# Projections, output weights, gate, up and down in four tiles of 32 columns of TensorE's array

## The reference, cut to what matters

```
x = x + attention(layernorm(x))
x = x + ffn(layernorm(x))

attention: q, k, v = split_heads(x @ W.T + b)       # 16 heads of 16
           q, k = rope(q), rope(k)
           att = softmax(causal mask of q @ k.T / 4)
           (att @ v) @ Wo.T + bo
ffn:       gate, up = fp4_linear(x, w_gate), fp4_linear(x, w_up)     # 256 -> 704
           fp4_linear(silu(gate) * up, w_down)                       # 704 -> 256
fp4_linear(x, w): both rounded to an FP4 grid in blocks of 16, then x @ w.T
```

## Time and profile before

| | us |
|---|---|
| median of 3 runs | 1334.23 |
| the profiled execution's own time | 1329.79 |
| its span, first to last instruction | 1327.6 |
| TensorE (PE) busy | 1266.5 |
| VectorE (DVE) busy | 1088.6 |
| ScalarE (ACT) busy | 792.5 |
| GpSimd (POOL) busy | 472.1 |

### The profile page before, as it was taken

How to read it: one execution, slowest core, us unless ns; L and a number is a source line. 1 busy time by engine, 2 the same in 40 slices (tenths; PEclk the granted TensorE clock), 3 DMA queues, 4 the chain that set the end, 5 groups by cost and what they waited for, 6 DMA issues and landing times.

```text
span 1327.6 us, 43992 instructions
## 1 busy us (share of the span) xinstructions
PE 1266.5 (95%) x19062; PEld 821.1 (62%) x19062; DVE 1088.6 (82%) x2242; ACT 792.5 (60%) x1691; POOL 472.1 (36%) x499
## 2 busy tenths in 40 slices
PE   7679999999999999999999999999999999999967
PEld 6456555555666775666576766566765676855445
DVE  5788898989899897986468979889998898984256
ACT  5346667666567665675655647555665585766621
POOL 2944664653112203113355651313122312023346
PEclk9879999999999999999999999999999999999989
DMA  4634132202110110101023222111100100000000
GB/s 107 171 93 114 51 86 70 80 19 58 34 34 2 42 27 18 27 3 43 13 66 90 62 67 57 34 34 34 26 18 26 42 2 14 7 1 18 13 13 16
DMA packets 56988, 57.54 MB, mean 43 GB/s; under 512 B 10062, under 2 KB 50384, under 8 KB 56784
## 3 DMA queue, kind: packets, MB, share of 16 engines
q1 hardware_dynamic: 55496, 53.66, 15.0%
q10 hardware_dynamic: 1300, 1.08, 0.3%
HBM read 37.55 MB, written 16.78 MB: 41 GB/s over the span
## 4 chain that ended last, share of the span: by engine, by line
PE 76%; DVE 15%; ACT 3%; POOL 3%; issue 2%; DMA 1%; SPq 0%; ACTq 0%; POOLq 0%; DVEq 0%
PE bank L906 16%; PE bank L860 15%; PE bank L883 14%; PE bank L918 13%; DVE piece_max L1282 7%; PE bank L1038 5%; PE bank L978 4%; ACT prob L1182 2%; PE bank L986 2%; PE bank L1029 1%; PE bank L913 1%; PE bank L887 1%; PE bank L866 1%; DVE c_mem L1354 1%; DVE c_mem L1344 1%
## 5 line engine op out<-in xcount | busy, mean ns | idle before, releaser
L1182 ACT ACTIVATE prob<-bank 128x512 f32<-128x512 f32 (+3 forms) x1280 | 605.2, 539 | 280.5 <-PE bank L883 160.2
L1282 DVE TENSOR_REDUCE piece_max<-bank 128x1 f32<-128x512 f32 (+3 forms) x1120 | 690.3, 662 | 26.3 <-PE bank L860 11.9
L860 PE MATMUL bank<-k_mem,q_mem 96*32 96x512 bf16 (+3 forms) x5120 | 441.2, 351 | 7.3 <-DVE piece_max L1282 4.8
L883 PE MATMUL bank<-q_mem,k_mem 99*32 99x512 bf16 (+3 forms) x5120 | 443.6, 349 | 4.3 <-DVE piece_max L1282 2.4
L906 PE MATMUL bank<-prob,V 128*32 128x512 f32 (+3 forms) x2560 | 309.2, 531 | 6.6 <-ACT prob L1182 6.0
L883 PEld LDWEIGHTS bank<-q_mem,k_mem 99*32 99x32 bf16 x5120 | 190.2, 96 | 124.0 <-issue 63.1
L860 PEld LDWEIGHTS bank<-k_mem,q_mem 96*32 96x32 bf16 x5120 | 188.5, 97 | 116.3 <-issue 63.5
L1490 POOL TENSOR_TENSOR c_mem<-c_mem 128x256 f32<-128x256 f32 (+2 forms) x74 | 85.5, 1156 | 474.9 <-DVE c_mem L1366 474.9
L887 PE MATMUL bank<-mask_kq,ident_h 128*32 128x128 bf16 (+3 forms) x2048 | 129.8, 200 | 0.0
L866 PE MATMUL bank<-mask_qk,ident_h 128*32 128x32 bf16 (+3 forms) x2048 | 116.6, 203 | 0.0
L906 PEld LDWEIGHTS bank<-prob,V 128*32 128x32 f32 x2560 | 84.4, 110 | 42.0 <-ACT prob L1182 17.6
(11 more groups left out here) (174 smaller groups left out, 1412.8 us busy)
## 6 DMA issues: line engine op xcount, KB each, us to landing
parts_dram<-a_mem SPq DMA_DIRECT2D x13, 512.0 KB, 3.3
q_mem<-parts_dram SPq DMA_DIRECT2D x32, 192.0 KB, 2.9
k_mem<-parts_dram SPq DMA_DIRECT2D x32, 192.0 KB, 3.5
q_mem<-parts_dram SPq DMA_DIRECT2D x32, 128.0 KB, 3.1
k_mem<-parts_dram SPq DMA_DIRECT2D x32, 128.0 KB, 3.4
c_mem<-in_L_attn_x SPq DMA_DIRECT2D x30, 128.0 KB, 2.1
out<-c_mem SPq DMA_DIRECT2D x30, 128.0 KB, 1.7
a_mem<-in_L_attn_x SPq DMA_DIRECT2D x13, 256.0 KB, 2.6
```

Source lines behind the costliest of these rows:

```text
L860: m = pe.matmul(b[q0:q0 + COLUMNS, j * keys:(j + 1) * keys], q_rows(u)[0:TERM_ROWS, h, i * P + q0:i * P + q0 + COLUMNS], k_rows(k0 // CHUN ...
L883: mm = pe.matmul(b[k0:k0 + COLUMNS, off:CHUNK], k_rows(j // TPC, g)[:, h, first:first + COLUMNS], q_rows(u)[:, h, off:CHUNK], start=True, ...
L1182: act.activation(prob[:, n % NP, off:CHUNK], bank_of("st", n)[:, off:CHUNK], ACT.Exp, scale=SCALE).then_inc(drained("st", n)[0], 1)
L1282: dve.tensor_reduce(piece_max[:, u % 2, h0:h0 + len(heads), slot], src.rearrange("p (h k) -> p h k", k=keys), AX.X, ALU.max).then_inc(drai ...
```

## The change

The five products that had a stationary operand of 128 columns are written as four matmuls with 32 columns each, for each of their parts of the contraction. The streamed operand of the four is the same, and each writes its own 32 partitions of the bank. The planner is told that these jobs are `divided`. The durations that it takes for them are left as they are, and so are all transposes, which it takes as not divided, the one of the maxima too.

```
-        plan.start(plan.through(("v", z), 1728, "dve", 600, [...], [("past v",), ("v bias load",)]), pair_sooner(z))
+        plan.start(plan.through(("v", z), 1728, "dve", 600, [...],
+                                [("past v",), ("v bias load",)], divided=True), pair_sooner(z))
...   (q and k, wo, g0, g1, u0, u1 and down: divided as well)
             def product(b, src, w, lo, width):
                 for d in range(DK):
-                    m = pe.matmul(b[:, 0:width], src[:, d * P:(d + 1) * P], w[:, d, lo:lo + width],
-                                  start=(d == 0), stop=(d == DK - 1))
+                    for t0 in range(0, P, COLUMNS):
+                        m = pe.matmul(b[t0:t0 + COLUMNS, 0:width], src[:, d * P + t0:d * P + t0 + COLUMNS],
+                                      w[:, d, lo:lo + width], start=(d == 0), stop=(d == DK - 1))
                 return m
...   project_features
-                    for d in range(DK):
-                        m = pe.matmul(b[:, a * SIDE:(a + 1) * SIDE], WqkvT[:, d, o * D + a * P:o * D + (a + 1) * P],
+                    for d, f0 in ((d, f0) for d in range(DK) for f0 in range(0, P, COLUMNS)):
+                        of = o * D + a * P + f0
+                        m = pe.matmul(b[f0:f0 + COLUMNS, a * SIDE:(a + 1) * SIDE], WqkvT[:, d, of:of + COLUMNS],
                                       A[a_set[z]]["xnT"][:, d, :], start=(d == 0), stop=(d == DK - 1))
...   project_v: the same over i and d
...   down
-                for j in range(len(DOWN)):
-                    m = pe.matmul(b[:, 0:D], hT[0:DOWN[j], j * P:(j + 1) * P], WdT[0:DOWN[j], j, :],
-                                  start=(j == 0), stop=(j == len(DOWN) - 1))
+                for j, t0 in ((j, t0) for j in range(len(DOWN)) for t0 in range(0, P, COLUMNS)):
+                    m = pe.matmul(b[t0:t0 + COLUMNS, 0:D], hT[0:DOWN[j], j * P + t0:j * P + t0 + COLUMNS],
+                                  WdT[0:DOWN[j], j, :], start=(j == 0), stop=(j == len(DOWN) - 1))
```

More of the change, by code:

```diff
@@ L309, in rehearse_projection @@
                                     [("drain", "bias")] + old("lo"),
-                                    ("act", (name + "0", z), 285, ("drain", "bias"), *old("lo"))), pair_sooner(z))
+                                    ("act", (name + "0", z), 285, ("drain", "bias"), *old("lo")), True), pair_sooner(z))
         plan.start(plan.through(("v", z), 1728, "dve", 600, [("drain", "xnT", z), ("drain", "aw", 2)],
-                                [("past v",), ("v bias load",)]), pair_sooner(z))
+                                [("past v",), ("v bias load",)], divided=True), pair_sooner(z))
         for n, name in enumerate(("cos load", "sin load")):
@@ L472, in rehearse_feed_forward @@
         yield from plan.step("pool", ("residual", t), 685, [("f x load", t), ("bo load",)])
-        yield from plan.through(("wo", t), 864, "dve", 342, [("drain", "yT", t)], [("residual", t)])
+        yield from plan.through(("wo", t), 864, "dve", 342, [("drain", "yT", t)], [("residual", t)], divided=True)
         yield from plan.step("dve", ("f stats", t), 335, [("drain", "wo", t)])
@@ L482, in rehearse_feed_forward @@
             yield from plan.through((f"g{half}", t), 1184, "dve", 430, [("drain", "xT", t)], [],
-                                    ("act", ("tanh", half, t), 360) + ((("drain", "g0", t),) if half else ()))
-            yield from plan.through((f"u{half}", t), 1184, "dve", 435, [("drain", "xT", t)], [("drain", f"g{half}", t)])
+                                    ("act", ("tanh", half, t), 360) + ((("drain", "g0", t),) if half else ()), True)
+            yield from plan.through((f"u{half}", t), 1184, "dve", 435, [("drain", "xT", t)], [("drain", f"g{half}", t)], divided=True)
         yield from rehearse_rounding(("h", t), FF, [("drain", "u1", t)])
@@ L487, in rehearse_feed_forward @@
         yield from plan.through(("hT1", t), 220, "act", 265, [("grid", 2, "h", t)])
-        yield from plan.through(("down", t), 2590, "dve", 349, [("drain", "hT0", t), ("drain", "hT1", t)])
+        yield from plan.through(("down", t), 2590, "dve", 349, [("drain", "hT0", t), ("drain", "hT1", t)], divided=True)
         yield from plan.load("sp", ("store", t), 128, [("drain", "down", t)])
@@ L984, in project_v @@
                 for i in range(PAIR):
-                    for d in range(DK):
-                        m = pe.matmul(b[:, i * D:(i + 1) * D], A[a_set[z]]["xnT"][:, d, i * P:(i + 1) * P],
+                    for d, t0 in ((d, t0) for d in range(DK) for t0 in range(0, P, COLUMNS)):
+                        m = pe.matmul(b[t0:t0 + COLUMNS, i * D:(i + 1) * D],
+                                      A[a_set[z]]["xnT"][:, d, i * P + t0:i * P + t0 + COLUMNS],
                                       WqkvT[:, d, 2 * D:3 * D], start=(d == 0), stop=(d == DK - 1))
```

## The result

The changed kernel took 1352.76 us (median of 4 runs, 1351.35 to 1353.61) against 1336.11 for the kernel before on the same chip: ratio 1.0127, with a 95% interval of 1.0105 to 1.0148. It is slower by 17 us, where 12 us faster was predicted; the time lies outside the range. Its profiled execution has a span of 1350.7 us, 23.1 over the one before.

The account below looks back on a forecast made before the run. TensorE was taken as the bound, busy 1266.5 of 1327.6 us. 12.7 - 2.4 + 1.5 = 11.8, less a tenth 10.6, plus 1 for smoother order: 11.6, say 12; 1334 - 12 = 1322 us, range 1308 to 1336.

Parts of the forecast that it names:

- The mechanism of the saving: On TensorE, streaming stays equal; the gain is in changes of kind, 0.29 us per products-only stretch, 0.24 per transpose stretch.
- Removed: On PE in the old order, 53 products-only stretches vanish and 31 mixed ones become 46 of transposes: net 12.7 us saved.
- added: Product instructions go from 1408 to 5632; late first sets cost 0.01 us per product, 2.4 us, bounds 0 and 4.8.
- Moved: the order: Planner's new order gives 134 undivided transpose stretches instead of 140: 1.5 us gained, bounds 10 us more to 8 less.
- The prediction's own sign of being wrong: PE's idle time from 133 to 1195 us above 20 us, with DVE (VectorE) named.
- What shorter stretches do elsewhere: Products between scores smooth ScalarE and VectorE work: 1 us won of PE's 10.5 us idle; a tenth off the other terms.
- The gain is taken up by the others: Rival: VectorE at 90% or late feed-forward tiles eat the 12 us, giving 1330 to 1334; 23%.
- Four small matmuls can't keep the array fed: Rival: each set of four on TensorE comes late by 0.02 us, +15 to +21 us, up to 1355; 7%.
- the chance of 8% for slower: Slower outcomes together: 7% for late sets of four, 1% for tiles of 32 columns not running concurrently.

Follow-up runs that it names:

- the old order: Products in four tiles as in the changed kernel, the planner told what it was told before, so every job keeps its place: 1328.1 us, ratio 0.9943.
- two other orders: Kernel before with the planner's norm preference 200 to 0: 1351.87 us, PE idle 25.3 us; and the changed kernel's order: 1352.76 us, idle 33.6 us.
- an order sought for either kernel: Planner preferences found by letting the planner alone try some hundreds: changed kernel 1308.01 us, ratio 0.9802; kernel before, undivided, 1327.15 us, ratio 0.9948.
- the run with fillers in these waits: Changed kernel, same order, with identity multiplications on TensorE in five waits behind which the clock fell: 1348.88 us, ratio 1.0113.

## Why the prediction was wrong

*The mechanism of the saving was right.* Streaming takes the same time for four tiles as for the whole array (1.18 us for gate or up, 0.86 for the output weights); a change of kind costs 0.09 us in, 0.15 or 0.20 within and out; 140 stretches remain in the old order. "Removed" and "added" gave 10.3 us, and with the order held the runs give 5 to 10, 9.6 in PE's busy time.

*The step that failed is "Moved: the order".* I treated the new order as the old one with a different number of stretches and took 1.5 us of gain, bounds 8 and 10 us for the count alone. The count came out as forecast (130 for 134) and said nothing: the order cost 25 us, 19 of them waits of PE. It was read as a matter of change-overs, where it is one of when each job stands against the engines that feed it. PE's 10.5 us of idle time were looked at only as what a better order could win; an order with so little has more room to be worse, and two other orders put it at 15 and 23 us more. Which property of an order makes these waits stays open.

What could have been seen beforehand is the planner's own end. It needs no run, and the change moves it from 1309.8 to 1327.6 us, 17.8 later, where the kernel became 17 us slower; the planner knows nothing of what the tiles save, so the agreement is in part luck. Its preferences act on every job after the first one moved, so the old order's fit isn't carried over, and that order was a good one: of the six values of BESIDE_NS above, its 2000 gives the kernel before its earliest end.

The prediction's own sign of being wrong, over 20 us of PE's idle time from 133 to 1195 us, came (33.6), but not as described: VectorE ended 9 us of it, and ScalarE, DMA and GpSimd the rest.

*"What shorter stretches do elsewhere"* had the wrong sign: 1 us of idle time was to be won. With the order held PE's idle time rose by 8 us (18.4 for 10.5), in the new order by 23, and there ScalarE did 11 us less by 600 us.

*The rivals.* "The gain is taken up by the others" named waits and late tiles, but priced them at 12 us at most. Waiting was nearest to what happened, at half the 25 us it cost; late tiles weren't it, since four were left after the last values, as before. "Four small matmuls can't keep the array fed" gave 1349 to 1355, nearly the measured time, by a cause that didn't occur: without the runs in the old order it would have passed for the explanation. A rival on the slower side whose mechanism is the order itself was missing, and the chance of 8% for slower was that of the wrong rival. The tail stayed near 60 us as forecast (61 us, 1289.5 to 1350.7).

## What to carry to other kernels

Where a program or a greedy planner makes the order, a change to a job's cost or kind is two changes: predict the piece with the order held, and give the new order a spread of its own, taken from what small changes of the planner's inputs do to its end. Measure the two halves apart before the idea is dropped: here the idea was worth 7 us in the old order and 19 us with an order sought for either kernel (26 against the kernel before as it was), and the change as made lost 17. Look at the planner's end before the first run: within the tiled kernels, and within the undivided ones, its rank was that of the measured times as far as the runs can tell them apart. PE's idle time had that rank in the tiled kernels; the count of change-overs had it in neither.

## What the runs showed of the hardware

Sixteen fp32 matmuls of 32 stationary columns with one streamed operand of 352 columns pass in 1.18 us, as four of 128 do.

The granted clock fell to half (1.2 of 2.4 GHz) in the body of the changed kernel behind PE waits of only 2.2, 1.4 and 2.1 us (ended at 302.4, 903.6 and 1085.0 us), which I hadn't reckoned with. The fall from 357.9 us is on record 0.4 us before the wait of 3.9 us began, behind two of 0.5 and 0.7. Waits of the same length at 140.7 us (2.3) and 720.2 (1.4) had no fall, so the length alone doesn't decide it. In the run with fillers in these waits the body had no fall, but the clock fell in places of the tail where it hadn't before. Taking the falls away moved the whole time by no more than the runs can tell, though in the tail gate and up at full clock brought the last down 2.1 to 2.4 us sooner.
